# Edge loop of a graph attention kernel: each engine takes the oldest block's stage first

## The reference

```
q, k, v = x @ W.T + b            (per node, 4 heads x 16)
logits  = (q[dst] * k[src]).sum(-1) / 4
e       = exp(logits - segment_max(logits, dst)[dst])
alpha   = e / (segment_sum(e, dst)[dst] + 1e-16)
out     = segment_sum(v[src] * alpha, dst) + x @ Ws.T + bs
```

## Time and profile before

| | |
|---|---|
| median of 3 timed runs | 3456.58 us (3455.79 to 3459.07) |
| span of the profiled execution | 3819.9 us; no other figure of its time is given |
| PE, DVE, ACT, POOL busy, share of the span | 68%, 60%, 37%, 48% |
| edge phase 0, edge phase 1, about | 208 to 1442 us, 1603 to 2840 us |
| expert phase, about | 2840 to 3820 us |

### The profile page before, as it was taken

How to read it: one execution, slowest core, us unless ns; L and a number is a source line. 1 busy time by engine, 2 the same in 40 slices (tenths; PEclk the granted TensorE clock), 3 DMA queues, 4 the chain that set the end, 5 groups by cost and what they waited for, 6 DMA issues and landing times. The chain is left out here.

```text
span 3819.9 us, 47527 instructions
## 1 busy us (share of the span) xinstructions
PE 2598.0 (68%) x13194; PEld 2196.2 (57%) x13194; DVE 2277.4 (60%) x3441; ACT 1404.8 (37%) x2768; POOL 1847.1 (48%) x1956
## 2 busy tenths in 40 slices
PE   2446656666666563466666666666658999999999
PEld 1335445555545453344555445445547999899998
DVE  3236666656766672266666666666655655566655
ACT  6212222222222221022222222222226666676665
POOL 6466666666666646666666666666631000000000
PEclk9755666665566665556666666666658999999999
DMA  9344444434444432344444444444420000000000
GB/s 379 100 102 116 113 112 120 116 110 115 118 112 120 113 93 48 84 110 119 121 123 120 122 119 119 124 114 124 120 76 15 21 5 19 23 11 12 20 10 11
DMA packets 364547, 356.12 MB, mean 93 GB/s; under 512 B 58787, under 2 KB 297682, under 8 KB 364454
## 3 DMA queue, kind: packets, MB, share of 16 engines
q1 hardware_dynamic: 191798, 168.12, 14.0%
q0 software_dynamic: 62832, 125.63, 13.4%
q10 hardware_dynamic: 109824, 61.36, 5.4%
HBM read 246.63 MB, written 108.30 MB: 93 GB/s over the span
## 5 line engine op out<-in xcount | busy, mean ns | idle before, releaser
L154 POOL DMA_INDIRECT kv<-kv_table,ix x1664 | 1582.6, 951 | 842.5 <-issue 468.5
L618 DVE TENSOR_TENSOR_SCAN held_q<-mask,held_q,qT 128x512 f32<-128x512 bf16 x208 | 264.1, 1270 | 785.3 <-remote 733.8
L590 PE MATMUL outT<-identity,run_v 128*128 128x128 f32 x832 | 321.7, 387 | 513.6 <-ACT rows L677 434.1
L568 PE MATMUL kT<-identity,kv 128*128 128x128 f32 x832 | 353.6, 427 | 429.7 <-DMA kv<-kv_table,ix 311.1
L590 PEld LDWEIGHTS outT<-identity,run_v 128*128 128x128 f32 x832 | 219.1, 263 | 573.2 <-ACT rows L677 415.0
L662 ACT ACTIVATE drop<-rise 128x512 f32<-128x512 f32 x208 | 130.9, 629 | 935.6 <-DVE rise L638 478.4
L568 PEld LDWEIGHTS kT<-identity,kv 128*128 128x128 f32 x832 | 193.2, 232 | 446.4 <-issue 375.2
L1245 ACT ACTIVATE full_x<-psH_x,offset_x,scale_x 128x448 f32<-128x448 f32 x448 | 333.6, 745 | 260.3 <-PE psH_x L1098 253.0
L1372 DVE TENSOR_TENSOR hid_lo_x<-full_x,hid_hi_x 128x448 fp32r<-128x448 f32 x448 | 276.1, 623 | 253.4 <-ACT hid_hi_x L1245 242.8
L575 PE MATMUL logit<-kq,head_sum 128*128 128x512 f32 x416 | 389.4, 1039 | 22.6 <-issue 15.8
L592 PE MATMUL restT<-pick,top 128*128 128x8 f32 x1664 | 394.5, 310 | 0.0
(11 more groups left out here) (223 smaller groups left out, 5556.6 us busy)
## 6 DMA issues: line engine op xcount, KB each, us to landing
running_sums<-rows ACTq DMA_DIRECT2D x208, 288.0 KB
qz<-q_at_starts SPq DMA_DIRECT2D x208, 256.0 KB
mask<-masks SPq DMA_DIRECT2D x416, 128.0 KB
q_at_starts<-zeros SPq DMA_DIRECT2D x16, 1664.0 KB
kv<-kv_table,ix POOLq DMA_INDIRECT x1664
x_sb<-in_x SPq DMA_DIRECT2D x1, 6272.0 KB
kv_table<-proj SPq DMA_DIRECT2D x14, 448.0 KB
x_x<-in_x POOLq DMA_DIRECT2D x7, 896.0 KB, 5.7
```

The lines of the kernel that those rows point to most:

```text
L154: pool.indirect_dma_start(kv[:, b % UNROLL, j, 2 * HC * s:2 * HC * (s + 1)], None, kv_t, bass.IndirectOffsetOnAxis(ix[:, b, n:n + 1], 0)). ...
L568: pe.transpose(kT[u % 2][:, P * j:P * (j + 1)], kv[:, u, j, 0::2], identity[:, :])
L590: pe.transpose(outT[:, of], run_v[:, u, of], identity[:, :])
L618: dve.tensor_tensor_scan(held_q[:, h, :], mask[:, u, 0, :], qT[:, :], held_q[:, 1 - h, STEP - 1:STEP], ALU.mult, ALU.add).then_inc(q_held, 1)
```

## The change

Every engine that goes through `each_block` takes its stages in reverse: the one with the largest lag, which belongs to the oldest block, first, and the one of the newest block last. TensorE's round becomes turn_results(r-3), turn_v(r-2), logits(r-1), turn_kq(r); VectorE's sums(r-2), maximum(r-1), hold_q(r); ScalarE's store(r-2), weights(r). The rounds at the end are reversed in the same way. Waits, counts, buffers, SP and POOL are as before.

```diff
+                def oldest_first(stages):
+                    return [(lag, stages[lag]) for lag in range(len(stages) - 1, -1, -1)]
+
                 def each_block(eng, stages, before=None, after=None):
...
                     def blocks(i):
                         for u in range(U):
-                            for lag, stage in enumerate(stages):
+                            for lag, stage in oldest_first(stages):
                                 b = U * i + u - lag
                                 if not isinstance(i, int) or b >= U * past:
                                     stage(b, (u - lag) % U, i if u >= lag else i - 1)
                     each_step(eng, body)
                     for late in range(1, len(stages)):
-                        for lag in range(late, len(stages)):
+                        for lag, stage in oldest_first(stages)[:len(stages) - late]:
                             b = U * (past + STEPS) + late - 1 - lag
-                            stages[lag](b, b % U, b // U)
+                            stage(b, b % U, b // U)
```

## The result

| | before | after |
|---|---|---|
| median | 3456.06 us (20 runs) | 3447.22 us (20 runs) |
| ratio, 95% interval | 1 | 0.9972 (0.9963 to 0.9981) |
| span of the profiled execution | 3819.9 us | 3447.0 us |
| POOL's pauses at a block's head, "remote" | 374.0 us | none |
| kT(103) to the next phase's first gather | 30.6, 30.9 us | 26.9, 26.6 us |

The ratio says 0.28%, 9.7 us (6.6 to 12.8; the medians differ by 8.8), clear of no change by the interval and small. One of the 20 runs of before took 3640 us, 5% more than the others, and stays out of the ratio. The spans say 373 us, and that is no effect of the change: this kernel was met at two levels of time. Before takes 3456 us here, and it took 3838 to 3867 us on each of the four chips of the experiments, where the change made no difference of 0.3% either way (experiments 5 and 11). I call these the first and the second kind of chip.

What follows compares the result with a forecast made beforehand. POOL's gather cadence, 10.05 us a block, was taken to bound the edge loops. Steady loop 0 plus two drains of -3.4 us made -7: 3456.6 to 3450 us; own range 3446 to 3453, eight in ten 3415 to 3464.

Steps and rivals of the forecast that it cites:

- The bound: Edge loops: POOL's 8 gathers of 1.255 us set 10.05 us a block, 2090 us of the 3456.
- The late increments: TensorE's increments reach other engines 6 us and more late; taken as mostly the profiled execution's own, absent from timed runs.
- a longer slack removes most of them: POOL's pauses in the profiled execution: if increments stay late, most go and the span falls towards 3477 us.
- The sign that I had named for being right: POOL's "remote" row, its wait before the gathers, falls well below 374 us.
- No gain in the steady loop: Edge loops: POOL takes 10.05 us a block in both orders, so the change brings 0 us.
- rival C: Loop slower: two 7.9 us circuits tied to one turn per block, plus late increments; 3508 or 3540 us; chance 0.13.
- The slack of POOL: POOL's release by turn_v in the loop comes earlier, its slack growing from 2.9 to 10.6 us.
- VectorE's and TensorE's schedule: One loop round: turn_v ends at T'+6.9, sums at 9.9, hold_q starts about 12.6; VectorE idles 2.3 us per block.
- The drain: End of each edge phase: turn_results(103) starts at 17.9 instead of 21.75 us; 3.4 us gained per phase, bounds 2 and 5.
- ScalarE "priced at 0": Second layer, store behind part_high: copies done T'+19.5, wanted T'+22.0; 0 us, bounds 0 and 48 us.
- Rival A: Timed runs still hold POOL pauses that the slack removes: 3320 to 3390 us, or 3415 to 3440; chance 0.17.

Runs made afterwards that it cites:

- experiment 5: The changed kernel itself, run again beside the kernel before on a slower chip: ratio 1.0006 (0.9987 to 1.0025).
- 11: The changed kernel once more on another chip: 3869.15 us against 3865.67 for the kernel before, ratio 1.0007.
- 2: The changed kernel with one gather buffer less, POOL waiting for turn_v of block b-3: 3827.59 us, 0.9973 of the kernel before.
- 4: The kernel before with only VectorE's stages reversed, TensorE and ScalarE in the old order: 3872.38 us, ratio 1.0087.
- 6: The changed kernel with the old order kept in the rounds at the end, only the loop reversed: ratio 1.0025 to the kernel before.
- 7: The changed kernel with the old order kept in the loop, only the rounds at the end reversed: ratio 1.0056 to the kernel before.
- 10: The same kernel as 7, run again on another chip: ratio 1.0076 to the kernel before.
- 9: The changed kernel with POOL making 4 of 8 gathers from block 4 on: 3161.0 us, 0.8176 of the kernel before.
- 1: The kernel before with one gather buffer less, POOL waiting for turn_v of block b-3: 4739.74 us, ratio 1.2346.
- experiment 8: The changed kernel with ScalarE left in the old order, TensorE and VectorE reversed: 4331.79 us, 1.128 of the kernel before.
- 12: The kernel before with POOL making 4 of 8 gathers from block 4 on: 3036.36 us, ratio 0.7849.
- 3: The kernel before with only TensorE's stages reversed, VectorE and ScalarE in the old order: 4974.55 us, ratio 1.2958.

## Why the prediction was right, and where it was not

**The bound** (POOL's cadence, 10.05 us a block, in the timed runs): right for the timed runs, and shown by the profile of after. For before at this level there is no trace; that its loop runs at the cadence too follows from the times alone, which leave it 0.06 us a block at most (12.8 us over 208).

**The late increments:** wrong in their attribution. I took the lateness to be the profiled execution's own. But timed runs of before took 3838 to 3867 us on the chips of the experiments: there POOL's pauses are time that was measured, whatever causes them. And the forecast that a longer slack removes most of them, with a span towards 3477 us, failed: with the order of after and the lateness present, "remote" stayed at 374.5 us (experiment 5):

```profile
POOL kv L154 <- remote: 374.5, 186, 4.5
```

The sign that I had named for being right, this row well below 374, and the span of 3447.0 us came by luck: the trace of after is from the other kind.

**No gain in the steady loop:** right on both kinds. On the second the reason is another than I gave, and it is not settled. In the profile of experiment 5 (TensorE, then VectorE, then POOL, of one round):

```profile
1016.87 0.47 PE L593 MATMUL outT<-identity,run_v 128*128 128x128 f32 x1 [3.66 <-DVE run_v L654]
...
1020.73 1.09 PE L584 MATMUL vT<-identity,kv 128*128 128x128 f32 x4
...
1023.35 0.42 PE L571 MATMUL kT<-identity,kv 128*128 128x128 f32 x1
```

```profile
1025.51 0.69 DVE L647 TENSOR_TENSOR wv<-vT,ex 128x512 f32<-128x512 f32 x1 [4.08 <-remote]
```

```profile
1022.73 0.95 POOL L154 DMA_INDIRECT kv<-kv_table,ix  x1 [0.30 <-issue]
1025.68 0.95 POOL L154 DMA_INDIRECT kv<-kv_table,ix  x1 [1.99 <-remote]
```

turn_v ended at 1021.8 and VectorE saw it at 1025.5, 3.7 us late. On the circuit turn_v, sums, turn_results of 7.9 us that gives 11.6, the measured period, and it looks like rival C. But that sum is no proof, since the lateness is read from the same rows. Two things speak against it: the period is 11.63 to 11.75 us in before and in 2, 4, 5, 6, 7, 10 and 11, whose circuits differ, and with half the gathers the lateness was gone (9). What fits them better is a block of 8 gathers (9.75 us to the end of the last) and then increments of turn_v that arrive only 1.7 to 1.9 us after that end (medians of 2, 5, 11 and before). POOL is released with VectorE, so the slack that the change bought is of no use. C's price did not come: before pays the same, and neither side wins. This is argued, and no run isolates it.

**The slack of POOL** (2.9 to 10.6 us): right. Experiments 1 and 2 show that a block of slack was won. In the trace of after the first gather of a block starts 11.8 us after the turn_v that frees its buffer at the median, 11.2 at the least, so the slack there is about 11 us at the least. **VectorE's and TensorE's schedule:** right within 0.2 us. **The drain:** 3.4 us forecast, 3.6 and 4.3 in the traces, 3.9 in the mean; two of them make 7.9 of the 9.7 us, and the interval holds that. The stages behind kT(103) came as summed; that the reversed loop alone would bring all of the gain (the expectation of 6) did not hold. That the whole gain on the first kind lies in the drains is inferred: its trace of before is missing.

**ScalarE "priced at 0":** right, in value and in working: in the trace of after TensorE never waits for the copies. In layer two part_high and the store behind it were forecast to end at T'+19.5 and to be wanted at T'+22. In the round of T' = 1710.16 the copies end at T'+20.0 and turn_results starts at T'+21.95, 1.9 us later; over the 24 such rounds the margin is 1.1 to 3.7 us. (The T+12 of experiment 8 belongs to its own expectation, where the copies stand behind weights.)

```profile
1728.90 0.63 ACT L689 ACTIVATE expert_w_hi<-w_raw 128x512 f32 x1 [3.78 <-DMA w_raw<-in_expert_w]
1729.44 0.58 ACT L677 ACTIVATE rows<-outT 128x512 f32<-128x512 f32 x1
1729.92 0.28 ACT L680 ACTIVATE rows<-restT 128x32 f32<-128x32 f32 x2
...
1732.11 0.42 PE L593 MATMUL outT<-identity,run_v 128*128 128x128 f32 x1
```

**Rival A** (pauses in the timed run, tens of microseconds) did not come on the first kind: 9.7 us. On the second there were some 320 to 350 us of pauses, and the change removed none of them.

**Open:** what makes the two levels, the chip or something else. One rival that no run tests is the recording of the execution itself. The traces of the second kind hold far fewer records of the gathers' landing (822 to 4351 for one kv semaphore, against 6633 to 6651 in the trace of after, for the same number of gathers in all but 9 and 12), so a jam of such records may be what holds the increments up. Open are also, for the first kind, direct readings of experiments 6 and 7. No version with all of the gathers beats both kernels: on the first kind only before and after were measured, and after is the faster; on the second none is better than before beyond 0.3% (2 comes nearest, at 0.9973, and 5, with one buffer more, at 1.0006 on another chip; no reason for a difference was found).

## What to carry to other kernels

In a software pipeline the order of the stages within a round decides how many rounds lie between an event and what it releases, not how much work there is. Where another queue sets the pace, a better order shows only at the ends, as here 4 us each; but it may make a buffer superfluous. All engines have to be reversed together: on the second kind of chip ScalarE left behind cost 12.8% (8), VectorE and ScalarE 29.6% (3), and VectorE reversed alone 0.9% (4). The last would be more where a block takes 10.05 us: its 11.7 us a block make some 340 us over 208 blocks, an estimate from these two periods. Before a gap between a profile and the timed runs is put down to the profiler, the kernel before should be timed on more than one chip. And a sign that the forecast was right counts only if both traces were taken under the same conditions.

## What the runs showed of the hardware

POOL issued a gather each 1.255 us; the median from one start to the next is 1.256 to 1.260 us in every trace, on both kinds of chip.

On the second kind TensorE's increments can reach the other engines late: by 3.5 us at the median for turn_v in experiment 5, and by up to 16.5 us for turn_results in the trace of before (the earlier trace rows show waits of 12), and several arrive within 0.2 us of each other. In the one trace of the first kind, with the program of experiment 5, they come within 0.01 to 0.02 us. In experiments 1, 3, 8 and 9 on the second kind they were in time too; there POOL paused 3.5 us and more per block or made half the gathers. Where POOL's pauses were under 2 us at the median and all gathers were made they were late, save in 4, where those of turn_v lagged by 0.2 us. In 5 those of turn_v came 1.4 to 1.9 us after the end of POOL's last gather. That back-to-back gathers hold the increments up would fit all this; which is cause and which effect wasn't separated. With half the gathers and pauses of 2.6 us at the median the lateness in the order of before (12) was 0.7 us or less at the upper quartile for turn_v.
